# GRU step on TensorE: where the two transposes of the state stand among the products

## What is computed

```python
def cell(h, x):                      # h, x: [128, 256]; 32 steps, one after the other
    gi = x @ W_ih + b_ih             # [128, 768]
    gh = h @ W_hh + b_hh
    i_r, i_z, i_n = jnp.split(gi, 3, axis=-1)
    h_r, h_z, h_n = jnp.split(gh, 3, axis=-1)
    r = jax.nn.sigmoid(i_r + h_r)
    z = jax.nn.sigmoid(i_z + h_z)
    n = jnp.tanh(i_n + r * h_n)
    h_new = (1.0 - z) * n + z * h
    return (h_new, h_new)
xs = jnp.swapaxes(inputs, 0, 1)      # inputs: [128 batch, 32 steps, 256]
_, hs = jax.lax.scan(cell, initial_state, xs)
```

## Time and profile before

| what | value |
|---|---|
| median of 3 runs | 345.14 us |
| lowest and highest | 343.35 and 345.91 us |
| the profiled execution, its own time | 347.7 us |
| its span, first to last instruction | 345.5 us |
| TensorE busy over the span | 95% |
| attention part, up to the first products of the GRU | 196.4 us of the span |

### The profile page before, as it was taken

How to read it: one execution, slowest core, us unless ns; L and a number is a source line. 1 busy time by engine, 2 the same in 40 slices (tenths; PEclk the granted TensorE clock), 3 DMA queues, 4 the chain that set the end, 5 groups by cost and what they waited for, 6 DMA issues and landing times.

```text
span 345.5 us, 12266 instructions
## 1 busy us (share of the span) xinstructions
PE 327.8 (95%) x4182; PEld 296.1 (86%) x4182; DVE 251.4 (73%) x665; ACT 237.3 (69%) x721; POOL 224.2 (65%) x403
## 2 busy tenths in 40 slices
PE   8998879999999999999976999999999999999994
PEld 7767667888888888888865999999999999999994
DVE  2768859999999999999987366655556566665555
ACT  3778767788787888888655566666666666666662
POOL 5688667687787778779965345555555555555552
PEclk9999989999999999999999999999999999999999
DMA  6885644334333332333342221121111111111111
GB/s 198 288 250 145 187 137 138 94 81 122 117 115 95 118 102 80 116 115 104 110 121 69 68 71 47 61 64 61 61 51 56 46 60 61 61 61 61 61 59 35
DMA packets 32199, 34.06 MB, mean 99 GB/s; under 512 B 5286, under 2 KB 26796, under 8 KB 32172
## 3 DMA queue, kind: packets, MB, share of 16 engines
q1 hardware_dynamic: 26108, 26.30, 25.4%
q10 hardware_dynamic: 6064, 7.41, 6.7%
HBM read 12.46 MB, written 8.39 MB: 60 GB/s over the span
## 4 chain that ended last, share of the span: by engine, by line
PE 82%; SPq 8%; ACT 2%; DVE 2%; DMA 2%; issue 2%; POOL 1%; DVEq 0%; POOLq 0%; ACTq 0%
PE bank L1206 38%; PE bank L1163 20%; PE bank L1336 5%; PE bank L1317 4%; SPq L394 4%; PE bank L1305 4%; SPq L402 4%; PE bank L1436 3%; PE bank L1169 2%; DMA operands<-operands 2%; PE bank L1288 2%; PE bank L1297 2%; PE bank L1183 1%; PE bank L1246 0%; DVE probsT L1042 0%
## 5 line engine op out<-in xcount | busy, mean ns | idle before, releaser
L1206 PE MATMUL bank<-wih_lo,wo_parts 128*128 128x256 f32 x192 | 56.3, 294 | 0.0
L1206 PE MATMUL bank<-wih_hi,wo_parts 128*128 128x256 f32 x192 | 53.7, 281 | 0.0
L1206 PE MATMUL bank<-wih_hi,pair_lo 128*128 128x256 f32 x192 | 52.9, 280 | 0.0
L1206 PE MATMUL bank<-wqkv_hi,hT_hi 128*128 128x256 f32 x192 | 52.7, 293 | 0.0
L583 POOL TENSOR_TENSOR operands<-operands,h 128x128 f32<-128x128 f32 x64 | 29.6, 462 | 35.4 <-ACT operands L869 34.4
L1206 PE MATMUL bank<-wqkv_lo,hT_hi 128*128 128x256 f32 x192 | 50.1, 280 | 0.0
L1106 DVE TENSOR_TENSOR operands<-bank,operands 128x128 f32<-128x128 f32 x64 | 18.6, 291 | 39.8 <-ACT operands L866 39.8
L1163 PE MATMUL bank<-wqkv_hi,xn_hi 128*128 128x512 f32 (+1 forms) x124 | 46.6, 376 | 0.3 <-POOL xn_lo L505 0.3
L1206 PE MATMUL bank<-wqkv_hi,hT_lo 128*128 128x256 f32 x192 | 42.8, 279 | 0.0
L590 POOL TENSOR_TENSOR w_emb_sb<-h,w_emb_sb 128x256 f32<-128x256 f32 x31 | 22.7, 733 | 30.0 <-DVE h L1123 30.0
L1163 PE MATMUL bank<-wqkv_hi,xn_lo 128*128 128x512 f32 (+1 forms) x124 | 42.0, 338 | 0.0
(11 more groups left out here) (136 smaller groups left out, 984.7 us busy)
## 6 DMA issues: line engine op xcount, KB each, us to landing
v_diag<-v_rows SPq DMA_DIRECT2D x128, 34.0 KB, 1.9
operands<-operands SPq DMA_DIRECT2D x64, 64.0 KB, 2.0
operands<-operands SPq DMA_DIRECT2D x32, 128.0 KB, 2.1
out_dram<-x ACTq DMA_DIRECT2D x16, 256.0 KB, 2.5
w_emb_sb<-out_dram SPq DMA_DIRECT2D x32, 128.0 KB, 2.1
out_dram<-w_emb_sb SPq DMA_DIRECT2D x31, 128.0 KB, 1.7
x_in<-in_x_dram SPq DMA_DIRECT2D x7, 512.0 KB, 9.0
stage_w<-in_L_cond_W_ih_dram ACTq DMA_DIRECT2D x2, 384.0 KB, 4.8
```

The costliest lines, as they stand in the source:

```text
L1206: return pe.matmul(dst, moved, gate_columns(weights, k, block), start=False, stop=True, skip_group_check=True)
```

## The change

The number of input products ahead of the first transpose goes from 13 to 14, so four stand behind it, not five. The second transpose used to stand ahead of all state products; now one state product (high by high, block 0, half 0) stands ahead of it, with its wait for `hi_ready[0]`. The two products of `state_high(e, 0, 0)` are written out for that. No instruction is added or taken away, and no other engine's queue is touched.

```diff
-FIRST_INPUTS = 13
+FIRST_INPUTS = 14
...
                 turned(0)
                 for block, k, term in inputs[FIRST_INPUTS:]:
                     input_term(e, pair_slot, block, k, term)
+
+                pe.wait_ge(hi_ready[0], t + 1)
+                add_product(state_block(e, 0), hT_hi[:, 0, :], wqkv_hi, 0, 0)
                 turned(1)
-
-                pe.wait_ge(hi_ready[0], t + 1)
-                state_high(e, 0, 0)
+                add_product(state_block(e, 0), hT_hi[:, 0, :], wqkv_lo, 0, 0)
                 state_high(e, "n", 0)
                 pe.wait_ge(lo_ready[0], t + 1)
                 state_low(e, 0, 0)
```

## The result

| | before | after |
|---|---|---|
| median of 7 runs each | 345.15 us | 347.92 us |
| lowest and highest | 343.35 and 345.91 us | 347.20 and 349.06 us |
| ratio | | 1.0076, 95% interval 1.0053 to 1.0098 |
| profiled execution, its own time | 347.7 us | 348.55 us |
| first to last load of `turned(0)`, 30 periods | 200.63 to 337.82 us | 198.93 to 338.59 us |

The change makes the kernel slower by 0.76% (the ratio), which is 2.6 us; the two medians are 2.8 us apart. Two spans alone would mislead: 345.5 and 346.3 us are only 0.8 us apart, because in the profile after the attention part, which the change doesn't touch, came to the first transpose of the GRU 1.7 us sooner. The thirty periods of the GRU are 2.47 us longer (139.66 against 137.19).

The account below looks back on a forecast made before the run. The prediction took a ring from h half 0 through transposes, products and gates as the bound. The product behind the second cast comes 0.08 us later per step: 31 x 0.08 = 2.5 us, 345.14 + 2.5 = 347.6 us, range 344.9 to 349.2.

Parts of the forecast that it names:

- The first transpose's wait goes, but is no gain: First transpose one product later: its wait goes to about nothing, but a new 0.15 us wait eats the 0.10 won.
- The exposed load: State product ahead of the second transpose: its time from load to slot, hidden before, now shows, taken as 0.10 us.
- the rival of an even result: State product starts as soon after its load as a transpose (0.06 us), changes cancel: 345.4 us, chance 0.17.
- The second cast: ScalarE's cast behind the second transpose ends at 252.40, before 252.23; the product waiting for it is 0.08 us later.
- ScalarE's queue: Copies behind the second cast move by 0.17 us; queue and TensorE both release r's sigmoid at 253.33, no extra cost.
- The full gain: Rival: first transpose's wait goes and no new one comes, 31 x 0.10 = 3.1 us, 342.0 us; chance 0.05.
- a waiting load that would hold back the next one: Within a rival of chance 0.10: second transpose's load also held back, 0.14 us per step, 349.4 us.

Follow-up runs that it names:

- e1: Kernel before with 14 instead of 13 input products ahead of the first transpose, second transpose still ahead of all state products: 343.76 us, ratio 0.9965.
- e6: Changed kernel with the second transpose one product later still, behind two state products: 351.36 us, ratio 1.0172 to the kernel before.
- e5: Changed kernel with the second of set_gates' two copies moved from ScalarE to VectorE: 347.71 us, ratio 1.0064 to the kernel before.
- e4: Changed kernel, product ahead of the second transpose using the step's input instead of the state, cast wait behind that transpose: 344.02 us, ratio 0.9966 to before.
- e3: Kernel before with 12 instead of 13 input products ahead of the first transpose: 348.45 us, ratio 1.0108.

## Why the prediction was right

The forecast was 347.6 us, slower by 0.7%; measured were 347.92 us and 0.76%, and the waits were where the forecast had them. The steps, as times from the first transpose's load:

| step of the forecast | forecast | measured |
|---|---|---|
| slot of the first transpose | 0.08 | 0.07 |
| end of its cast | 0.66 | 0.65 |
| load and slot of the first state product | 0.71, 0.81 | 0.70, 0.81 |
| slot of the second transpose | 0.93 | 0.93 |
| slot of the next state product | 1.05 | 255.94 - 0.117 = 255.82: 1.03 |
| end of the second cast | 1.51 | 1.50 |
| load and slot of the product behind it | 1.56, 1.66 | 1.55, 1.67 |
| longer per step | 0.08 | 0.082 |
| sum over 31 steps | 2.5 | 31 x 0.082 = 2.5 |

*The first transpose's wait goes, but is no gain.* Right: its load comes 0.04 behind the slot of the product ahead, and the product behind the cast waits for 0.15. By itself (e1) the wait went one place further, to the second transpose, and left 0.036.

*The exposed load.* The one number without a row in the GRU of the kernel before was the time from a released load to the slot, 0.10 from a pair in the attention part. It was 0.11 (255.49 to 255.60). The transposes' 0.06, on which the rival of an even result rested, doesn't hold for this form.

*The second cast.* Right, and e6 is the test of it: a slot later costs a slot.

*ScalarE's queue.* Its release and TensorE's were forecast for the same instant, at no cost. In the timeline after, the second copy starts at 252.06 and the sigmoid at 252.59:

```profile
252.06 0.59 ACT L691 COPY bank<-biases 128x512 f32<-128x512 f32 x1
...
252.59 0.28 ACT L866 ACTIVATE operands<-bank 128x128 f32<-128x128 f32 x1
```

That is 0.53 apart, the queue's own pace, so the row itself can't tell which of the two released it. e5 can: nothing is lost there.

*The full gain.* It would have needed the cast 0.17 sooner. e4 takes that wait away by other data, and the same order is then faster than the kernel before. It also shows the size: 0.07 in most steps and 0.054 in the mean, not 0.10, since the second cast and GpSimd's part of the inputs stand right behind.

*What was worked out less well.* Part of the chance of 0.22 for slower by over 1% stood on a waiting load that would hold back the next one, 0.14 per step. Nothing of the kind was seen: the transpose behind the waiting product sits in the very next slot, 0.12 later. The forecast also named no order that would be faster, though its own numbers held one: left ahead of the state products, the second transpose waits only until 251.55 (half 1 of h at 251.50 and 0.05 of signal) and is in slot 251.61 (0.06 from load to slot), where it was at 251.65. That is e1.

The Trainium skill's price for a load (TensorE: Matmul & The Clock Gate, LDWEIGHTS (loading the stationary operand): columns / 1.2 in ns, so 0.107 us for 128) is near the 0.11 that the state product took from its released load to its slot. For a transpose, which loads 128 columns too, the page would give the same, and the trace has 0.06 to 0.07 (254.79 to 254.86). The Trainium skill's rule that loads are pulled ahead of running matmuls (TensorE: Matmul & The Clock Gate, Step-by-step: what each phase is for) says nothing of a load whose data aren't there yet: the one at 255.49 came 0.05 behind the end of its cast. With that rule alone the change would have come out even, and it didn't.

## What to carry to other kernels

When a loop is a ring through several engines, don't count the waits on the busiest one. Follow the ring from the value that is ready last, and ask of each edit whether it puts an instruction into the ring or takes one out. Work ahead of a waiting instruction is free as long as it fits into the wait, and work behind it costs its whole slot where nothing further on waits (0.117 in e3, 0.113 in e6). A wait that is removed can come back at the next thing that isn't ready, as in e1 and e4. By these runs, an instruction that others wait for over a longer way (here a transpose, then a cast) should stand in the queue at the first slot at which its data are there, and ahead of anything that has a wait of its own.

## What was not expected of the hardware

Products don't always follow at the same pace at full clock. In e1 (timeline of TensorE, granted clock 1.00) fourteen slots from 248.80 to 250.38 take 1.58 us, 0.113 each, where 0.117 to 0.118 is usual:

```profile
248.80 0.39 PE L1206 MATMUL bank<-wqkv_hi,hT_lo 128*128 128x256 f32 x2
...
250.38 0.28 PE L1206 MATMUL bank<-wih_hi,wo_parts 128*128 128x256 f32 x1
```

Most of e1's steps have a period of 4.54 to 4.58 from one second transpose to the next, and until 290 us every fourth has 4.47; there the 32 products take 3.70 where the step shown above has 3.78. The kernel before has one such step of thirty, of 4.50, and the changed one has none. The cause was not looked into and stays open; it is no part of the changed kernel's loss, but it is a part of e1's gain. The five short steps are 0.10 shorter than the 4.573 of before, which is 0.5 us of the 1.08 us by which e1's thirty periods are shorter; a step of 4.54 gains the 0.03 that was expected.

At the shorter periods the next wait can be seen as well. In e1 GpSimd's low part of the next pair of inputs is finished at 254.84 and the first product that stands behind the wait for it loads at 254.89:

```profile
253.53 1.31 POOL L572 TENSOR_TENSOR pair_lo<-x2T,wo_parts 128x512 fp32r<-128x512 f32 x1
...
254.89 0.19 PEld L1206 LDWEIGHTS bank<-wih_hi,wo_parts 128*128 128x128 f32 x1
```

Its load was due at 254.82 (0.117 behind the one at 254.70), so it is 0.07 late. In e4, six of the thirty steps, every fourth up to 310 us, are 4.58 instead of 4.50, and it is the same wait. One of them:

```profile
254.67 1.29 POOL L572 TENSOR_TENSOR pair_lo<-x2T,wo_parts 128x512 fp32r<-128x512 f32 x1
...
255.81 0.19 PEld L1206 LDWEIGHTS bank<-wqkv_hi,hT_lo 128*128 128x128 f32 x1
256.02 0.19 PEld L1206 LDWEIGHTS bank<-wih_hi,wo_parts 128*128 128x128 f32 x1
```

The low part is finished at 255.96, and the load that was due at 255.93 comes at 256.02. In all six the load stands 0.20 to 0.21 behind the one before it. The changed kernel has no such wait: its loads at this place stand 0.12 behind the one before, and at least 0.12 behind GpSimd's end.
